# Two layer norms and four small jobs move from VectorE to ScalarE, and decayed reads stay in PSUM, in a gated delta-rule attention kernel with a mixture-of-experts layer

## The chip, the cores and the metric

One core of a Trainium2 chip (trn2) runs one program. The metric is the device time of that program in microseconds (us). The engines are TensorE (PE; PEld is its weight load), VectorE (DVE), ScalarE (ACT), GpSimd (POOL) and SyncE (SP, the DMA queue). Each runs its own instruction stream in order and meets the others only at semaphores.

## The reference

One transformer layer over 4096 tokens of width 256, in fp32. First comes a linear attention with 8 heads and 8 modes per head, then a top-2 mixture of 8 experts.

```python
h = layernorm(x) * (1 + ca) + sa
q, k, v = h @ Wq, h @ Wk, h @ Wv                   # 8 heads of 64
beta, tg = sigmoid(h @ Wbeta), sigmoid(h @ Wtg)    # per head and mode
rho = exp(-softplus(log_decay)); g = log(clip(tg * rho, 1e-6))
# q, k rotated by pos * exp(omega_log_scale) * inv_freq, unit length
for t in range(T):                                 # per head and mode
    S = S * exp(g[t])
    dv = (v[t] - k[t] @ S) * beta[t]
    S = S + outer(k[t], dv)
    y[t] = q[t] @ S
o = einsum(y, softmax(mode_logits)) * sigmoid(h @ Wg)
x = x + ga * (o @ Wo)
h2 = layernorm(x) * (1 + cb) + sb
x = x + gb * moe(h2)                               # top 2 of 8, capacity 1024
```

## The kernel before

The attention runs over 32 tiles of 128 tokens. A tile is done in two halves (`hh` = 0 and 1), each with 8 of the 16 "quads" of head and mode. Half `u = 2n + hh` works on two things at once. It builds its own chunk systems: angles, rotated keys and queries, decays, Gram matrices, and a triangular inverse for 4 chunks of 32 tokens. And it runs the recurrence of the half before it, `v = u - 1`, chunk by chunk. `memories(step, c)` in VectorE's `half` marks the recurrence steps; c is the chunk.

One chunk of the recurrence is a chain over engines. PE reads the memories (`memory_read`, L572) into `bank_mem[g]`, g = 0 and 1. VectorE scales that read by the decay (L1263) and subtracts it from the values (L1266): `right_sides`. PE multiplies by the inverse (L589) and adds the reads of the outputs (L595): `corrections`. VectorE scales by `dec_end` (L1273), PE forms the update (L608), POOL fades the state (L1561) and VectorE adds (L1282).

The work of the half itself is placed between those steps by hand. What the change touches sits here:

- `beta_decays` (L1199) first copies the last decay of each chunk into `dec_end` (L1201), then makes `bd` (L1205), just ahead of the fourth `right_sides`.
- At the end of a half VectorE runs `solve` (L1234): a transpose (L1236), 31 elimination steps j of two instructions each (L1245, L1247), a transpose into `tt` (L1250). `meanwhile` puts small jobs between the steps.
- In an hh = 1 half `tile_norm(n + 1)` (L1096) comes before `solve`: ScalarE's square root (L788), reciprocal (L1098), normalised rows `xn` (L1099). PE's `tile_front` turns `xn`, ScalarE makes `hT` (L753, L755) and the sigmoid `sg` (L759), and inside the same `solve` VectorE runs `clip_decays` at j = 8 (L1104 copies the betas, L1105 clips), `sum_decays` at j = 16 (the scan L1110, the spread over modes L1111) and `weigh_decays` at j = 24 (L1116).
- In an hh = 0 half `residual(n - 1)` (L1291 to L1295) and `second_norm(n - 1)` (L1297: square root L870 on ScalarE, L1299, `xn2` L1301) come before `solve`. PE's `route` (L633, L638) turns `xn2`, ScalarE makes `h2T` (L896), PE makes the router's logits, and VectorE takes them at j = 12 of that `solve` (`take_logits`, L1306).
- ScalarE's `roots` (L793) takes the squared lengths that PE sums in `sum_squares` (L490) from POOL's `squares` (L1552): a logarithm (L798) and an exponential (L799). POOL starts that work after `pw_raw`, which VectorE raises after the residual: L1586, two products and a sum (L1523, L1526), then `squares`.

ScalarE loads a function table (ACT_TABLE_LOAD) where two functions of different tables follow each other. After the tile loop come the routing of all tokens and the experts' matmuls, which the change does not touch.

Of the kernel before, what the change touches and what calls it, by code (L numbers as in the profile page):

```python
# [17 lines left out]
ALU = mybir.AluOpType  # L18
# [3 lines left out]
P = 128  # L22
# [101 lines left out]
def build(nc, x_in, Wq, Wk, Wv, Wbeta, Wtg, mode_logits, log_decay, omega_log, Wg, Wo,  # L124
# [12 lines left out]
    with outer, ctx:  # L137
        names = {}

        def sem(name):  # L140
# [8 lines left out]
            "vector": dict.fromkeys(["xn_ready", "xn2_ready", "dve_bank_free0", "dve_bank_free1", "state_ready0", "state_ready1",  # L149
# [4 lines left out]
            "scalar": dict.fromkeys(["act_bank_free0", "act_bank_free1", "hid_ready0", "hid_ready1",  # L154
# [151 lines left out]
        V_STEPS = (95, 190)  # L306
# [122 lines left out]
        def _(pe):  # L429
# [226 lines left out]
            def half(n, hh, first=False, last=False):  # L656
# [71 lines left out]
        def _(act):  # L728
# [19 lines left out]
            def tile_front(n):  # L748
# [10 lines left out]
                take(lambda b: act.activation(sg[:], b[:, 0:P], ACT.Sigmoid))  # L759
# [24 lines left out]
            def front(n, hh):  # L784

                if hh == 0:
                    act.wait_ge(sem("var_ready"), n + 1)
                    act.activation(stat[:, 8:9], stat[:, 7:8], ACT.Sqrt, bias=eps_ln[:]).then_inc(sem("std_ready"), 1)  # L788
                    tile_front(n)
# [3 lines left out]
            def roots(n, hh):  # L793
# [4 lines left out]
                take(lambda b: act.activation(rn[:].rearrange("p h t -> p (h t)"), b[:, :], ACT.Ln, bias=eps_l2[:]))  # L798
# [26 lines left out]
            def half(n, hh, first=False, last=False):  # L825
# [26 lines left out]
                act.activation(gc_end[:, hh], gc_end[:, hh], ACT.Exp).then_inc(sem("gc_end_ready"), 1)  # L852
                act.activation(eg_col[:, hh], col[:, :, 0, hh * HQ:hh * HQ + HQ], ACT.Exp).then_inc(sem("eg_col_ready"), 1)
# [14 lines left out]
                if hh == 0 and not first:  # L868
                    act.wait_ge(sem("var2_ready"), n)
                    act.activation(stat2[:, 8:9], stat2[:, 7:8], ACT.Sqrt, bias=eps_ln[:]).then_inc(sem("std2_ready"), 1)  # L870
# [10 lines left out]
                if not last:  # L881
                    front(*after(n, hh))
                if hh == 0 and not first:
                    route(n - 1)
                if not last:
                    roots(*after(n, hh))
# [17 lines left out]
            front(0, 0)  # L904
# [14 lines left out]
            act.wait_ge(sem("var2_ready"), NT)  # L919
            act.activation(stat2[:, 8:9], stat2[:, 7:8], ACT.Sqrt, bias=eps_ln[:]).then_inc(sem("std2_ready"), 1)  # L920
# [5 lines left out]
        def _(dve):  # L926
# [169 lines left out]
            def tile_norm(n):  # L1096
                dve.wait_ge(sem("std_ready"), n + 1)
                ln(dve.reciprocal(stat[:, 9:10], stat[:, 8:9]))  # L1098
                vec(dve.tensor_scalar(xn[:], xt[:], stat[:, 6:7], stat[:, 9:10], ALU.subtract, ALU.mult), "xn_ready", n + 1)  # L1099

            def clip_decays(n):
                dve.wait_ge(sem("sg_ready"), n + 1)
                dve.wait_ge(sem("rho_ready"), 1)
                ln(dve.tensor_copy(gb[64:128, :], sg[64:128, :]))  # L1104
                vec(dve.tensor_scalar(sg[0:64, :], sg[0:64, :], rho[0:64], 1e-6, ALU.mult, ALU.max), "tg_clipped", n + 1)  # L1105

            def sum_decays(n):
# [3 lines left out]
                vec(dve.tensor_tensor(xg[:], gb[:].rearrange("p (c j) -> p c j", c=NC).unsqueeze(2).broadcast_to([P, NC, 4, C]),  # L1111
                                      of_mode.unsqueeze(1).unsqueeze(3).broadcast_to([P, NC, 4, C]), ALU.mult), "spread_ready", n + 1)

            def weigh_decays(n):
                dve.wait_ge(sem("eg_raw"), n + 1)
                vec(dve.tensor_scalar(ew[0:64, :], ew[0:64, :], w_col[0:64], None, ALU.mult), "eg_ready", n + 1)  # L1116


# [80 lines left out]
            def beta_decays(u, hh):  # L1199
                dve.wait_ge(sem("dec_ready"), u + 1)  # L1200
                ln(dve.tensor_copy(dec_end[:, hh], dec[:, :, :, C - 1]))  # L1201
# [50 lines left out]
            def right_sides(v, hh, c):  # L1252
# [6 lines left out]
                for g in range(2):  # L1259
# [36 lines left out]

            def second_norm(t):  # L1297
                dve.wait_ge(sem("std2_ready"), t + 1)
                ln(dve.reciprocal(stat2[:, 9:10], stat2[:, 8:9]))  # L1299
                dve.wait_ge(sem("rows_sent"), since("rows_sent", t))  # L1300
                vec(dve.tensor_scalar(xn2[:], xr[:], stat2[:, 6:7], stat2[:, 9:10], ALU.subtract, ALU.mult), "xn2_ready", t + 1)  # L1301
# [72 lines left out]
            def half(n, hh, first=False, last=False):  # L1374
# [62 lines left out]
            tile_norm(0)  # L1437
            clip_decays(0)
            sum_decays(0)
            weigh_decays(0)  # L1440
# [403 lines left out]
```

## Time and profile before

| | us |
|---|---|
| time, 3 runs | 7270.02, 7274.76, 7275.66; median 7274.76 |
| profiled execution: its time | 7273.93 |
| its span | 7272.2 |
| busy PE, PEld | 4621.0 (64%), 3991.4 (55%) |
| busy DVE | 5425.6 (75%) |
| busy ACT | 3286.5 (45%) |
| busy POOL | 2786.6 (38%) |
| mean granted TensorE clock | 0.793 |

Busy times count what an engine executed, not its waits. "Granted clock" is the share of TensorE's full clock that the chip gave it. A timeline row has the start, the duration, engine, line, operation, output<-inputs with their shape, and in brackets the idle time before it with what ended that idle time. A group row has the count, the busy sum, the mean ns of one, and the idle time before them. Times inside the rows are microseconds from the span's start.

### The profile page before, as it was taken

To read this page: it belongs to the slowest core of one execution; us is meant where nothing else is said; L and a number is where in the kernel's file an instruction comes from. 1 tells how busy PE (TensorE), PEld (TensorE's weight loads), DVE (VectorE), ACT (ScalarE), POOL (GpSimd) and SP (SyncE) were. 2 spreads that over 40 slices of the span, in tenths; PEclk is the share of its full clock that TensorE was granted. 3 is DMA by queue.
4 is the path that set the end of the run, shared out by engine and by line. 5 is a ranking of instruction groups with operands and counts; after the bars stand their busy time and mean duration, and the time that the engine had idled before them with its cause. 6 is when DMAs were issued, how large, how long until landed. Compare 5 with 4: busy or idle time off the path is not lost. (4 is left out here: it accounts for less than half of the span.)

```text
span 7272.2 us, 195759 instructions
## 1 busy us (share of the span) xinstructions
PE 4621.0 (64%) x78513; PEld 3991.4 (55%) x78513; DVE 5425.6 (75%) x10088; ACT 3286.5 (45%) x5497; POOL 2786.6 (38%) x1789
## 2 busy tenths in 40 slices
PE   1666666666666666666666666666666666664994
PEld 1555555556555555555655555655565555563662
DVE  4888888888888888888888888888888888883003
ACT  1445454445444455444544445454454444541220
POOL 3444343344433434434434344343443434433003
PEclk6778877778777787777877778778787777886997
DMA  2000000000000000000000000000000000002223
GB/s 85 2 5 5 5 5 5 5 5 5 2 5 5 5 5 5 5 5 5 5 2 5 5 5 5 5 5 5 5 5 2 5 5 5 5 25 93 69 69 101
DMA packets 77478, 109.70 MB, mean 15 GB/s; under 512 B 20576, under 2 KB 66208, under 8 KB 75424
## 3 DMA queue, kind: packets, MB, share of 16 engines
q1 hardware_dynamic: 67616, 71.42, 3.1%
q0 software_dynamic: 8960, 25.39, 1.2%
q8 instruction: 672, 11.01, 0.6%
q14 instruction: 230, 1.88, 0.1%
HBM read 57.89 MB, written 38.89 MB: 13 GB/s over the span
## 5 line engine op out<-in xcount | busy, mean ns | idle before, releaser
L1561 POOL TENSOR_TENSOR state<-state,gc_end 128x512 f32<-128x512 f32 x512 | 594.7, 1173 | 1647.8 <-PE bank L595 1607.4
L589 PE MATMUL bank<-rhs,te 128*64 128x64 f32 x8192 | 432.2, 262 | 1054.3 <-DVE rhs L1266 725.5
L589 PEld LDWEIGHTS bank<-rhs,te 128*64 128x64 f32 x8192 | 360.4, 170 | 1141.1 <-DVE rhs L1266 1092.4
L572 PEld LDWEIGHTS bank<-state,ke 128*64 128x64 f32 x16384 | 610.5, 159 | 385.9 <-issue 194.6
L572 PE MATMUL bank<-state,ke 128*64 128x64 f32 x16384 | 649.7, 247 | 265.1 <-DVE outT L1284 171.7
L608 PE MATMUL last_two<-dvs,kte 128*64 128x64 f32 x16384 | 699.7, 250 | 179.3 <-DVE dvs L1273 179.3
L766 ACT ACTIVATE te<-tt 32x256 f32<-32x256 f32 x1024 | 421.9, 412 | 815.6 <-DVE tt L1250 805.1
L608 PEld LDWEIGHTS last_two<-dvs,kte 128*64 128x64 f32 x16384 | 637.7, 163 | 195.5 <-DVE dvs L1273 186.4
L1247 DVE TENSOR_TENSOR last_two<-last_two,prod 128x31 f32<-128x31 f32 (+15 forms) x1984 | 692.8, 349 | 68.1
L808 ACT ACTIVATE ke<-kq 32x512 f32<-32x512 f32 x1024 | 642.8, 628 | 198.6 <-DVE kq L1197 184.9
L1245 DVE TENSOR_TENSOR prod<-bd,last_two 128x31 f32<-128x31 f32 (+15 forms) x1984 | 670.6, 338 | 69.9
L533 PE MATMUL bank<-kq,ke 128*64 128x64 f32 x16384 | 615.7, 245 | 123.3 <-DVE pw L1232 112.0
L533 PEld LDWEIGHTS bank<-kq,ke 128*64 128x64 f32 x16384 | 594.5, 160 | 131.5 <-DVE pw L1232 77.2
L773 ACT ACTIVATE kte<-kt 32x512 f32<-32x512 f32 x1024 | 641.4, 626 | 15.8 <-PE last_two L608 1.9
L1586 POOL TENSOR_TENSOR pw<-pw,w_quad 128x1024 f32<-128x1024 f32 x64 | 122.4, 1913 | 1122.2 <-DVEq L1422 1122.2
L781 ACT ACTIVATE dv<-bank 128x256 f32<-128x256 f32 x512 | 188.5, 380 | 747.7 <-DVE dvs L1273 738.2
L508 PE MATMUL bank<-row_group,select 128*128 128x128 f32 x3072 | 431.2, 296 | 32.9 <-DVE col L1160 27.7
L1282 DVE TENSOR_TENSOR state<-last_two,state 128x512 f32<-128x512 f32 x512 | 354.0, 691 | 127.2 <-POOL state L1561 89.3
L508 PEld LDWEIGHTS bank<-row_group,select 128*128 128x128 f32 x3072 | 389.7, 203 | 52.4 <-DVE col L1160 28.0
L1756 DVE TENSOR_TENSOR yrow<-last_two,b_row 128x256 f32<-128x256 f32 x64 | 27.2, 425 | 508.5 <-PE last_two L1710 508.5
L595 PE MATMUL bank<-qg,state 128*64 128x32 f32 x8192 | 401.2, 249 | 0.0
L1574 POOL TENSOR_TENSOR tmp<-raw,cos_t 128x1024 f32<-128x1024 f32 x64 | 151.7, 2370 | 590.8 <-ACTq L849 590.8
(254 smaller groups left out, 10392.7 us busy)
## 6 DMA issues: line engine op xcount, KB each, us to landing
w_sb<-in_L_ffn_W_dram SPq DMA_DIRECT2D x16, 1024.0 KB, 9.4
expert_rows<-ke SPq DMA_DIRECT2D x1, 8192.0 KB, 21.9
xrows<-expert_rows SPq DMA_DIRECT2D x16, 512.0 KB, 8.4
expert_outputs<-yrow POOLq DMA_DIRECT2D x16, 512.0 KB, 3.4
xt<-_attn_hidden_states_dram SPq DMA_DIRECT2D x32, 128.0 KB, 2.1
xr<-_attn_hidden_states_dram SPq DMA_DIRECT2D x32, 128.0 KB, 2.1
x_after_attention<-xr SPq DMA_DIRECT2D x32, 128.0 KB, 1.7
xo<-x_after_attention SPq DMA_DIRECT2D x32, 128.0 KB, 3.6
```

What stands on the lines that cost most here:

```text
L508: mm = pe.matmul(b[:, ql * P:ql * P + P], select[:, b4 * 4 + ql, :], row_group[:, group, :], start=True, stop=True)
L533: mm = pe.matmul(b[s, q * 2 * C:(q + 1) * 2 * C], ke[:, c, r, q, s], kq[:, r, q, :, c * C:c * C + C], start=(r == 0), stop=(r == 1))
L572: mm = pe.matmul(bank_mem[g][s, q % 4 * DK:q % 4 * DK + DK], ke[:, c, r, q, s], state[:, hh * HQ + q, r, :], start=(r == 0), stop=(r == 1))
L589: pe.matmul(bank_mem[g][s, q % 4 * DK:q % 4 * DK + DK], te[:, q, s], rhs[:, q, :], start=True, stop=True)
L595: mm = pe.matmul(out_bank(g, side), state[:, hh * HQ + q, r, :], qg[:, r, q, c * C:c * C + C], start=(j == 0 and r == 0), stop=False)
L608: mm = pe.matmul(bank_upd[g][s, (q % 4) * P + r * DK:(q % 4) * P + r * DK + DK], kte[:, r, q, s], dvs[:, q, :], start=True, stop=True)
L766: ins = act.activation(te[s, :, 32 * m:32 * m + 32], tt[s, c, :, :], ACT.Copy)
L773: ins = act.activation(kte[s, :, :, 32 * m:32 * m + 32].rearrange("p r q f -> p (r q) f"), kt[s, :, :, c * C:c * C + C].rearrange("p r q f ...
L808: ins = act.activation(ke[s, c, :, :, 32 * m:32 * m + 32].rearrange("p r q j -> p (r q) j"), kq[s, :, :, 0, c * C:c * C + C].rearrange("p ...
L1245: ln(dve.tensor_tensor(pr, a_prob[:, j + 1:C, j:j + 1].broadcast_to([P, rows, cols]), t_prob[:, j:j + 1, 0:cols].broadcast_to([P, rows, co ...
L1247: ln(dve.tensor_tensor(below, below, pr, ALU.subtract))
L1561: pool.tensor_tensor(sv, sv, gc_end[:, vh, 4 * g:4 * g + 4, c].unsqueeze(2).broadcast_to([P, 4, 2 * DK]), ALU.mult).then_inc(sem(f"state_f ...
```

## The change

- `tile_norm` and `second_norm` run on ScalarE: ln(var + eps), the negated mean, exp of -0.5 times the logarithm, their product, and one Identity activation with scale and bias. VectorE keeps the statistics.
- `tile_norm(n + 1)` stands on ScalarE behind `clear_inverse`, ahead of the copies of the values. `second_norm(n - 1)` stands inside `roots`: its logarithm ahead of the logarithm of the lengths, the rest behind that.
- Since `route` needs `xn2`, it moves behind `roots` on ScalarE and behind `sum_squares` on PE. `take_logits` stays at j = 12 on VectorE.
- The sigmoid is split by partitions: decays' half to `sg`, betas' half straight to `gb`.
- ScalarE spreads the decays (four copies with a scale) and multiplies by the mode weights, behind its exponential of the summed decays.
- ScalarE copies `dec_end` behind its exponential of the decays.
- `right_sides` writes the scaled read back into `bank_mem[g]` and subtracts from there.

```diff
@@ PE and ScalarE, end of a half
-                if hh == 0 and not first:
-                    route(n - 1)
-                if not last:
-                    sum_squares(u + 1)
+                if not last:
+                    sum_squares(u + 1)
+                if hh == 0 and not first:
+                    route(n - 1)
...
+            def tile_norm(n):
+                act.wait_ge(sem("var_ready"), n + 1)
+                act.activation(stat[:, 8:9], stat[:, 7:8], ACT.Ln, bias=eps_ln[:])
+                act.activation(stat[:, 10:11], stat[:, 6:7], ACT.Copy, scale=-1.0).then_inc(sem("std_ready"), 1)
+                act.wait_ge(sem("std_ready"), 3 * n + 1)
+                act.activation(stat[:, 9:10], stat[:, 8:9], ACT.Exp, scale=-0.5).then_inc(sem("std_ready"), 1)
+                act.wait_ge(sem("std_ready"), 3 * n + 2)
+                act.activation(stat[:, 11:12], stat[:, 10:11], ACT.Copy, scale=stat[:, 9:10]).then_inc(sem("std_ready"), 1)
+                act.wait_ge(sem("std_ready"), 3 * n + 3)
+                act.activation(xn[:], xt[:], ACT.Identity, scale=stat[:, 9:10], bias=stat[:, 11:12]).then_inc(sem("xn_ready"), 1)
+            def second_norm(t, root=None):
+                act.wait_ge(sem("var2_ready"), t + 1)
+                act.activation(stat2[:, 8:9], stat2[:, 7:8], ACT.Ln, bias=eps_ln[:])
+                act.activation(stat2[:, 10:11], stat2[:, 6:7], ACT.Copy, scale=-1.0).then_inc(sem("std2_ready"), 1)
+                if root:
+                    root()
...
+                act.wait_ge(sem("rows_sent"), since("rows_sent", t))
+                act.activation(xn2[:], xr[:], ACT.Identity, scale=stat2[:, 9:10], bias=stat2[:, 11:12]).then_inc(sem("xn2_ready"), 1)
...
-                take(lambda b: act.activation(sg[:], b[:, 0:P], ACT.Sigmoid))
+                act.activation(sg[0:64, :], bank_act[turns.bank()][0:64, 0:P], ACT.Sigmoid)
+                take(lambda b: act.activation(gb[64:128, :], b[64:128, 0:P], ACT.Sigmoid))
...
                     act.wait_ge(sem("g_summed"), n + 1)
                     act.activation(ew[0:64, :], gb[0:64, :], ACT.Exp).then_inc(sem("eg_raw"), 1)
+                    for m in range(4):
+                        ins = act.activation(xg[:, :, m, :], gb[:].rearrange("p (c j) -> p c j", c=NC), ACT.Copy, scale=of_mode[:, m:m + 1])
+                    ins.then_inc(sem("spread_ready"), 1)
+                    act.wait_ge(sem("eg_raw"), n + 1)
+                    act.activation(ew[0:64, :], ew[0:64, :], ACT.Copy, scale=w_col[0:64]).then_inc(sem("eg_ready"), 1)
...
+                act.wait_ge(sem("dec_ready"), u + 1)
+                act.activation(dec_end[:, hh], dec[:, :, :, C - 1], ACT.Copy)
...
-                ln(dve.tensor_tensor(rhs[:, of], ksv, eg_col[:, hh, c, of].unsqueeze(2).broadcast_to([P, 4, DK]), ALU.mult))
+                ln(dve.tensor_tensor(ksv, ksv, eg_col[:, hh, c, of].unsqueeze(2).broadcast_to([P, 4, DK]), ALU.mult))
...
-                    vec(dve.tensor_tensor(r4, vv, r4, ALU.subtract), f"rhs_ready{g}", vc + 1)
+                    vec(dve.tensor_tensor(r4, vv, ksv.rearrange("p (h g) v -> p h g v", g=2), ALU.subtract), f"rhs_ready{g}", vc + 1)
...
-                if hh == 0 and not first:
-                    second_norm(n - 1)
-                if hh == 1 and not last:
-                    tile_norm(n2)
                 meanwhile = {}
                 if hh == 1 and not last:
-                    meanwhile.update({8: [lambda: clip_decays(n2)], 16: [lambda: sum_decays(n2)], 24: [lambda: weigh_decays(n2)]})
+                    meanwhile.update({8: [lambda: clip_decays(n2)], 16: [lambda: sum_decays(n2)]})
                 if hh == 0 and not first:
                     meanwhile[12] = [lambda: take_logits(n - 1)]
```

ScalarE's stream at the end of the loop's hh = 0 half, before: the take of `unit`, the two `h2T` of `route`, then the logarithm and exponential of `rn`.

```order
L790 ACTIVATE unit<-bank 128x512 [waits act_bank_full]
L745 REGISTER_ALU
L743 REGISTER_ALU [waits act_bank_free0]
L896 ACTIVATE h2T<-bank,mod_col 128x128 [waits act_bank_full]
L743 REGISTER_ALU [waits act_bank_free1]
L896 ACTIVATE h2T<-bank,mod_col 128x128 [waits act_bank_full]
L745 REGISTER_ALU
L743 REGISTER_ALU [waits act_bank_free0]
L798 ACT_TABLE_LOAD
L798 ACTIVATE rn<-bank,eps_l 128x512 [waits act_bank_full]
L799 ACT_TABLE_LOAD
L799 ACTIVATE rn<-rn 128x512 [waits act_bank_free1]
```

And with the change (`stat` is `stat2` and `xn` is `xn2` here; L763 to L773 are `second_norm`, L828 the logarithm and L833 the exponential of `rn`, L936 is `h2T`):

```order
L763 ACT_TABLE_LOAD [waits act_bank_free0]
L763 ACTIVATE stat<-stat,eps_ln 128x1 [waits var2_ready]
L764 ACTIVATE stat<-stat 128x1
L743 REGISTER_ALU
L828 ACTIVATE rn<-bank,eps_l 128x512 [waits act_bank_full]
L767 ISA [waits act_bank_free1]
L768 ACT_TABLE_LOAD
L768 ACTIVATE stat<-stat 128x1 [waits std2_ready]
L769 REGISTER_ALU
L770 ACTIVATE stat<-stat 128x1 [waits std2_ready]
L771 REGISTER_ALU
L773 ACTIVATE xn<-xr,stat 128x256 [waits rows_sent,std2_ready]
```

The activation that makes `xn2` now stands behind the logarithm of `rn`, and `h2T` behind both.

PE's stream at the same place, before:

```order
L555 MATMUL bank<-hT,wg_sb 128x128 x8
L452 REGISTER_ALU
L482 MATMUL bank<-hT,wqk_sb 128x128 x8
L633 MATMUL bank<-cmat,xn 128x128
L452 REGISTER_ALU
L633 MATMUL bank<-cmat,xn 128x128
L638 MATMUL bank<-wr_sb,h2T 128x8 x2
L490 MATMUL bank<-rhs,cmat 128x512
```

And with the change:

```order
L555 MATMUL bank<-hT,wg_sb 128x128 x8
L452 REGISTER_ALU
L482 MATMUL bank<-hT,wqk_sb 128x128 x8
L490 MATMUL bank<-rhs,cmat 128x512
L452 REGISTER_ALU
L633 MATMUL bank<-cmat,xn 128x128 x2
L638 MATMUL bank<-wr_sb,h2T 128x8 x2
```

The turning of `xn2` (L633) and the logits (L638) now stand behind `sum_squares` (L490).

## Rows read from the trace of the kernel before

**Rows 1.** The engines' busy time in three stretches: the tile loop, and two short ones.

```profile
core 0: us, PE busy (x) PEld busy (x) DVE busy (x) ACT busy (x) POOL busy (x), PEclk, DMA share, GB/s
100.00:6900.00 6800.00, 4351.37 (x77549) 3811.73 (x77550) 5303.26 (x9805) 3217.43 (x5396) 2697.61 (x1687) 0.79 0.03 10
3190.50:3195.50 5.00, 2.51 (x78) 2.40 (x79) 4.38 (x8) 4.88 (x9) 4.84 (x3) 1.00 0.01 3
3199.30:3203.00 3.70, 3.70 (x69) 3.58 (x67) 1.73 (x3) 2.20 (x5) 1.05 (x1) 0.50 0.02 4
```

**Rows 2.** A VectorE line that runs once a tile: durations, first and last start.

```profile
L1094 DVE TENSOR_SCALAR pos<-pos x3: 226/226/228, 2906.8 to 3309.5; 128x128 f32<-128x128 f32 x3
```

**Rows 3.** VectorE's groups by line and shape.

```profile
L1201 DVE COPY dec_end<-dec 128x32 f32<-128x32 f32 x64 | 66.9, 1045 | 9.6 <-DVE outT L1284 9.4
...
L1105 DVE TENSOR_SCALAR sg<-sg,rho 64x128 f32<-64x128 f32 x32 | 29.5, 921 | 1.1
...
L1247 DVE TENSOR_TENSOR last_two<-last_two,prod 128x256 f32<-128x256 f32 x64 | 27.6, 432 | 2.2
...
L1111 DVE TENSOR_TENSOR xg<-gb,cmat 128x512 f32<-128x512 f32 x32 | 22.1, 691 | 1.1
...
L1116 DVE TENSOR_SCALAR ew<-ew,w_col 64x128 f32<-64x128 f32 x32 | 8.9, 278 | 3.5 <-ACT ew L802 2.4
```

**Rows 4.** Line L1266 alone: duration in ns (min/median/max).

```profile
L1266 DVE TENSOR_TENSOR rhs<-v_sb,rhs x512: 424/425/2009, 230.8 to 6606.7; 128x256 f32<-128x256 f32 x171
```

**Rows 5.** Timeline, all engines, fourth chunk of a half (start us, us, what).

```profile
3194.84 2.41 POOL L1581 TENSOR_TENSOR kq<-tmp 128x1024 f32<-128x1024 f32 x1
...
3195.53 2.00 DVE L1266 TENSOR_TENSOR rhs<-v_sb,rhs 128x256 f32<-128x256 f32 x1
...
3199.31 3.66 PE L533 MATMUL bank<-kq,ke 128*64 128x64 f32 x64
...
3203.02 0.42 DVE L1231 TENSOR_TENSOR cos_t<-bank,bd 128x256 f32<-128x256 f32 x1 [1.92 <-PE bank L533]
```

**Rows 6.** Timeline, all engines, end of an hh = 1 half.

```profile
3115.16 0.42 DVE L1232 TENSOR_TENSOR pw<-bank,dec 128x256 f32<-128x256 f32 x1
...
3117.41 0.60 ACT L874 ACTIVATE v_sb<-bank 128x512 f32<-128x512 f32 x1 [1.13 <-PE bank L544]
...
3121.87 1.96 DVE L1236 STREAM_TRANSPOSE bd<-cos_t 128x1024 f32<-128x1024 f32 x1
...
3126.38 0.28 ACT L759 ACTIVATE sg<-bank 128x128 f32<-128x128 f32 x1
...
3129.58 0.94 DVE L1105 TENSOR_SCALAR sg<-sg,rho 64x128 f32<-64x128 f32 x1
```

**Rows 7.** Timeline, all engines, end of an hh = 0 half.

```profile
3017.40 0.18 DVE L1295 BATCH_NORM_AGGREGATE stat<-stat 128x2 f32<-128x6 f32 x1 [0.15 <-DVE stat L1293]
...
3019.81 2.01 DVE L1236 STREAM_TRANSPOSE bd<-cos_t 128x1024 f32<-128x1024 f32 x1
...
3026.09 1.04 POOL L1552 TENSOR_TENSOR rhs<-unit 128x512 f32<-128x512 f32 x1
...
3027.18 2.07 PE L490 MATMUL bank<-rhs,cmat 128*128 128x512 f32 x2 [1.49 <-POOL rhs L1552]
...
3029.30 0.69 ACT L798 ACTIVATE rn<-bank,eps_l 128x512 f32<-128x512 f32 x1 [2.87 <-PE bank L490]
...
3030.00 1.28 ACT L799 ACT_TABLE_LOAD   x1
...
3030.91 0.17 DVE L1306 TENSOR_TENSOR lg<-bank,br_row 128x8 f32 x1
...
3031.30 0.63 ACT L799 ACTIVATE rn<-rn 128x512 f32<-128x512 f32 x1
```

**Rows 8.** ScalarE's groups by line and shape.

```profile
L753 ACT ACTIVATE hT<-bank,mod_col 128x128 f32<-128x128 f32 x64 | 29.3, 457 | 90.4 <-PE bank L467 84.5 <-ACT hT L755 5.8
...
L870 ACT ACTIVATE stat<-stat,eps_ln 128x1 f32<-128x1 f32 x31 | 9.1, 294 | 234.8 <-DVE stat L1295 234.8
```

**Rows 9.** Timeline, the last tile's logits (idle before: from `xn2` on).

```profile
6624.51 0.17 DVE L1306 TENSOR_TENSOR lg<-bank,br_row 128x8 f32<-128x8 f32 x1 [2.60 <-PE bank L638]
```

More of the change, by code:

```diff
@@ L305, in build @@
         DVE_TURNS = (13, 26)
-        V_STEPS = (95, 190)
+        V_STEPS = (92, 185)
         G_STEPS = (29, 26)
@@ L746, in take, with tile_front @@
                 turns.next()
-            def tile_front(n):
+            def tile_norm(n):
[14 more added lines that the diff above has]
+                    root()
+                act.wait_ge(sem("std2_ready"), 3 * t + 1)
+                act.activation(stat2[:, 9:10], stat2[:, 8:9], ACT.Exp, scale=-0.5).then_inc(sem("std2_ready"), 1)
+                act.wait_ge(sem("std2_ready"), 3 * t + 2)
+                act.activation(stat2[:, 11:12], stat2[:, 10:11], ACT.Copy, scale=stat2[:, 9:10]).then_inc(sem("std2_ready"), 1)
+                act.wait_ge(sem("std2_ready"), 3 * t + 3)
+                act.wait_ge(sem("rows_sent"), since("rows_sent", t))
+                act.activation(xn2[:], xr[:], ACT.Identity, scale=stat2[:, 9:10], bias=stat2[:, 11:12]).then_inc(sem("xn2_ready"), 1)
+            def tile_front(n, first):
                 for k in range(KC):
@@ L758, in tile_front @@
                     act.sem_inc(sem("hT4_ready"), 1)
-                take(lambda b: act.activation(sg[:], b[:, 0:P], ACT.Sigmoid))
+                if not first:
+                    act.wait_ge(sem("groups_ready"), n)
+                act.wait_ge(sem("act_bank_full"), turns.uses() + 1)
+                act.activation(sg[0:64, :], bank_act[turns.bank()][0:64, 0:P], ACT.Sigmoid)
+                take(lambda b: act.activation(gb[64:128, :], b[64:128, 0:P], ACT.Sigmoid))
                 act.sem_inc(sem("sg_ready"), 1)
@@ L782, in take_dv, with front, roots @@
                                    ).then_inc(sem(f"dv_ready{g}"), 1)
-            def front(n, hh):
+            def front(n, hh, first=False):
                 if hh == 0:
-                    act.wait_ge(sem("var_ready"), n + 1)
-                    act.activation(stat[:, 8:9], stat[:, 7:8], ACT.Sqrt, bias=eps_ln[:]).then_inc(sem("std_ready"), 1)
-                    tile_front(n)
+                    tile_front(n, first)
                 take(lambda b: act.activation(unit[:].rearrange("p h t -> p (h t)"), b[:, :], ACT.Copy))
                 act.sem_inc(sem("raw_ready"), 1)
-            def roots(n, hh):
+            def roots(n, hh, t=None):
                 if hh == 0:
@@ L797, in roots, with logarithm @@
                     act.activation(gb[0:64, :], sg[0:64, :], ACT.Ln).then_inc(sem("g_ready"), 1)
-                take(lambda b: act.activation(rn[:].rearrange("p h t -> p (h t)"), b[:, :], ACT.Ln, bias=eps_l2[:]))
+                def logarithm():
+                    take(lambda b: act.activation(rn[:].rearrange("p h t -> p (h t)"), b[:, :], ACT.Ln, bias=eps_l2[:]))
+                if t is None:
+                    logarithm()
+                else:
+                    second_norm(t, logarithm)
                 act.activation(rn[:], rn[:], ACT.Exp, scale=-0.5).then_inc(sem("rn_root"), 1)
@@ L867, in half @@
                 clear_inverse(v, first)
-                if hh == 0 and not first:
-                    act.wait_ge(sem("var2_ready"), n)
-                    act.activation(stat2[:, 8:9], stat2[:, 7:8], ACT.Sqrt, bias=eps_ln[:]).then_inc(sem("std2_ready"), 1)
+                if hh == 1 and not last:
+                    tile_norm(n + 1)
                 if not first:
@@ L882, in half @@
                     front(*after(n, hh))
+                if not last:
+                    roots(*after(n, hh), t=n - 1 if hh == 0 and not first else None)
                 if hh == 0 and not first:
                     route(n - 1)
-                if not last:
-                    roots(*after(n, hh))
                 if not first:
@@ L902, in gaps @@
                 act.activation(per_tile[:, 5, t0:t1], per_tile[:, 4, t0:t1], ACT.Exp).then_inc(sem("gap_exp"), 1)
-            front(0, 0)
+            tile_norm(0)
+            front(0, 0, first=True)
             roots(0, 0)
@@ L918, in _ @@
                     next_expansions(v, c + 1)
-            act.wait_ge(sem("var2_ready"), NT)
-            act.activation(stat2[:, 8:9], stat2[:, 7:8], ACT.Sqrt, bias=eps_ln[:]).then_inc(sem("std2_ready"), 1)
+            second_norm(NT - 1)
             route(NT - 1)
@@ L1094, in tile_stats @@
                 ln(dve.tensor_scalar(pos[:], pos[:], float(P), None, ALU.add))
[L1096 to L1099, printed above, removed]
             def clip_decays(n):
@@ L1295, in residual @@
                 vec(dve.bn_aggr(stat2[:, 6:8], stat2[:, 0:6]), "var2_ready", t + 1)
[L1297 to L1301, printed above, removed]
             def take_logits(t):
```

14 lines of the change are left out of this document (2 added, 12 removed).

## The prediction

> **What bounds the kernel now.** I read the engines' busy times in stretches first. In the tile loop (100 to 6900 us) VectorE is busy 5303 of 6800 us, PE 4351, ScalarE 3217, POOL 2698 [rows 1]. One line that runs once a tile starts three times in 402.7 us, so a tile takes 201.35 us [rows 2], and 31 such tiles (each an hh = 1 half and the hh = 0 half of the next tile) make 6242 us of the span. Next I read the timeline of two halves, all engines together. VectorE has next to no gap there. Where it stands still, it is for a named partner: the Gram matrix of PE in the fourth chunk, 1.92 us [rows 5], and the square root ahead of the solve. So VectorE's own stream, with those waits, sets the time, and what leaves that stream counts in full until a partner becomes late. Each part is priced by asking who is late next.
>
> **First norm, end of the hh = 1 half.** Today L1232 ends at 3115.16 + 0.42 = 3115.58 and the transpose L1236 starts at 3121.87 [rows 6]. In the 6.29 us between lie a wait for ScalarE, a reciprocal and L1099. Afterwards nothing stands between the two but the usual 0.04: **6.25 us less**. Who could be late next is `clip_decays` at j = 8, which needs the sigmoid. Its turn comes at about 3123.1 (7.5 us into the solve, as today). On ScalarE the norm now stands ahead of the copies of the values, so `xn` is ready before PE asks for it; PE's turning, `hT` and the sigmoid follow the values directly. Today the sigmoid ends at 3126.66 [rows 6], some 4.8 us behind `xn`, which ends as L1236 starts; counted from the end of the last copy of the values (L874, 3118.01 [rows 6]) it ends near 3122.8. That just fits, and a miss costs tenths.
>
> **Small jobs in that solve.** L1111 (0.69 us) and L1116 (0.28) leave VectorE [rows 3]; the copy L1104 of the same 64x128 shape as L1116 leaves too and is taken at the same 0.28. With the gaps that is **1.3 us less**. L1105 stays. On ScalarE the spread is four copies of 128x128 with a scale, each at most the 0.46 of L753 [rows 8], so under 2 us. PE needs it for `columns`, but the scan that starts it comes 7 us sooner than today, so PE gets it sooner too. This costs nothing; were the cover gone, it would cost those 2 us a tile.
>
> **Fourth chunk, both halves.** The copy L1201 leaves VectorE: 1.05 us on average for 32 elements [rows 3]. It starts while POOL works and ends with POOL's instruction. The subtraction L1266 takes 0.42 us in the median and 2.01 at most [rows 4]; the long one is in the fourth chunk, starts at 3195.53 and ends at 3197.53, and POOL's L1581 ends at 3194.84 + 2.41 = 3197.25 [rows 5]. It reads two tensors from SBUF; afterwards it reads one from PSUM, like L1247, whose mean of 0.43 [rows 3] leaves no room for such waits. So VectorE gets 1.05 + 1.58 = 2.6 us. The partner behind is PE: its Gram matrix L533 starts at 3199.31 [rows 5], and it needs the rotated queries that L1581 makes. It can't start before 3197.3, so the path gets **2.0 us less in a half, 4.0 in a tile**. The bounds are 0 (another partner late) and 2.6 in a half; the row of POOL's end decides for 2.0. ScalarE's copy of `dec_end`, 32 elements, lies behind its exponentials, and its reader is a half away: nothing.
>
> **Writing the scaled read into its bank.** The same shape written to PSUM takes 0.432 us (L1247 [rows 3]) against 0.424 [rows 4]: 16 instructions a tile, **0.1 us more**.
>
> **Second norm, end of the hh = 0 half.** The statistics end at 3017.58; L1236 starts at 3019.81 [rows 7], and would start at 3017.61: 2.2 us less. But `take_logits` is still at j = 12 of this solve. Its turn was 3030.91 [rows 7] and would be 3028.7. The logits need `xn2`, and `xn2` now stands on ScalarE behind the logarithm of the lengths. That one waits for PE's sum (3027.18 to 3029.25), which waits for POOL's squares, which end at 3027.13 [rows 7] and hang on `pw_raw`; nothing in the change moves them. So: table load for the exponential from 3030.00, 1.28 us [rows 7]; two activations on one column at 0.29 each (L870 [rows 8], its like); one of 128x256, between 0.46 (128x128, L753 [rows 8]) and 0.69 (128x512, L798 [rows 7]), taken at 0.57; two waits of ScalarE for itself, an estimate of 0.17 each from VectorE's 0.15 ahead of L1295 [rows 7]. That makes `xn2` ready at 3032.8. From `xn2` to the logits the last tile shows 2.60 us [rows 9], so 3035.4. The solve stands still for 6.7 us at j = 12, and everything behind is 3035.4 - 3030.9 = **4.5 us later** than today instead of 2.2 sooner (bounds 3.9 and 5.3, by the ends of the terms). Behind this wait on VectorE is the rest of the elimination; nobody else gets late. SP's later store of `xn2` and load of `xr` have most of a tile to spare.
>
> The load L799 takes 1.28 us and a second one (L798's) stands just before it in the same tile. The Trainium skill, page "ScalarE: Activation LUTs", section "Table sets: the hidden batching unit", says that one set holds both exp and ln, so ln then exp would need a single load. By it the exponential's load would be missing and the time 31 x 1.28 = 40 us lower. The built stream has that load, and the trace disagrees with the rule. The same page, "What ACT_TABLE_LOAD costs", adds about 1.38 us of drain to the 1.28; by it the time would be 43 us higher. No such 1.38 us shows: L799's activation starts at 3031.30, 0.02 us behind the load [rows 7].
>
> **Sum.** Per tile -6.25 - 1.3 - 4.0 + 0.1 + 4.5 = -6.95 us; times 31 it is -215 us. The last hh = 1 half gives 2.0 more; the first and the last norm have nothing beside them and cost some 2.3 us each on ScalarE (a load more and two columns). Together -213. Against the profiled execution's 7273.93 us that is 7061, and against the median, 0.8 us above it, **7062 us**.
>
> **The rivals.**
> 1. *PE keeps its clock in the fourth chunk.* In 3190.5 to 3195.5 the granted clock is 1.00, and in 3199.3 to 3203.0 it is 0.50, where the Gram matrix takes 3.66 us; in between PE stood idle for want of L1266 [rows 1, 5]. If PE comes to it with shorter gaps and the clock stays up, L533 takes about half, and VectorE, which waits for it, gets up to 1.8 us more in each of 63 halves: 113 us, to 6950. Against it: PE still waits for POOL's queries, over a microsecond. 0.24.
> 2. *The fourth chunk gives nothing*, because another partner (`ke` on ScalarE, the update) takes the place: 63 x 2.0 = 126 us back, 7188. 0.10.
> 3. *The logits don't hold the solve*: 31 x 6.7 = 208 us less, 6854. This needs the squares to come 7 us sooner; their queue on POOL is unchanged. 0.05.
> 4. *One load for ln and exp*: 7022, by the row's 1.28 us for a load that falls away. Two loads show in the trace. 0.02.
> 5. *Slower: the logits' wait eats everything.* Place: L1306 at j = 12. Each microsecond that the logits come later than 3035.4 costs 31 us, so it decides from 3042.3 on, 6.9 us later than worked out; at 3044 the time is 7329. For it speaks that the chain from the sum of squares to the logits crosses between PE, ScalarE and VectorE six times and waits for itself on ScalarE, and each of these steps was taken from another place. Against it, no row shows such a step at over a microsecond beyond its work. The Trainium skill's same page, "Rules for kernel authors", wants multiply and add on VectorE, not on ScalarE, which speaks against the whole change. Here ScalarE is busy 47% of the loop and gets about 6 us of 201 more. 0.05.
> 6. *Nothing that can be measured* (gains and wait cancel): the wait would be 13.6 instead of 6.7 us. 0.02.
>
> **How the numbers follow.** The forecast has the remaining 0.52; its own range, from the bounds of the logits' term (3.9 to 5.3 us) and of the chunk's (1 to 2.6 us in a half), is 7005 to 7150. For 8 in 10 the range takes in rival 1 and its spread below and half of rival 2 above: 6930 to 7170. What a measurement of this kernel can tell from no change is about 0.2%, 15 us. Faster by more: 0.52 + 0.24 + 0.10 + 0.05 + 0.02 = 0.93; within: 0.02; slower: 0.05.
>
> **What would show it.** In the profile after, VectorE goes from its last `pw` to the transpose without a gap in hh = 1 halves; the logits' line waits some 6.5 us for PE in each of 31 tiles, near 200 us in all; the line after L1266 has a maximum near its median; the Gram matrix starts right behind POOL's last rotated sum; the line that runs once a tile comes every 194.4 us. I am wrong if the logits' wait is missing or over 10 us, or if the Gram matrix's wait grows by what the subtraction gave.

## The result and the profile after

| | before | after |
|---|---|---|
| time, median of 4 runs each | 7273.83 us | 7002.59 us (6999.14 to 7012.93) |
| ratio, 95% interval | | 0.963 (0.9616 to 0.9645) |
| span of the profiled execution | 7272.2 | 6997.4 |
| busy VectorE | 5425.6 | 5135.8 |
| busy ScalarE | 3286.5 | 3430.8 |
| busy PE | 4621.0 | 4452.0 |

The kernel is 271 us faster; 213 were forecast. Between the two profiled executions it is 274.8 us, and nearly all of that lies in the tile loop: from the first start of the transpose ahead of the solve to its last (64 starts, L1236 before, L1261 after) pass 6330.5 us before and 6059.7 after, 270.8 less. I call this the loop's time below. I compare by it where 10 us matter, since the experts' stage behind the loop, which no run touches, waits 504 to 509 us on one line in six of the profiled executions and 472 to 476 in the other eight (VectorE for PE's last products). The ratios below leave out two slow executions, one of `e6_before_bank_only` at 14515 us and one of `e9_sbuf_pe_kept_busy` at 7372.

VectorE's waits after (line waited for: us in all, times, longest):

```profile
DVE lg L1325 <- PE bank L638: 208.2, 32, 7.0
...
DVE cos_t L1256 <- PE bank L533: 85.3, 69, 6.9
...
DVE sg L1139 <- ACTq L791: 26.1, 16, 9.2
```

The first is the forecast one, 6.7 us in each of 31 tiles; 202.5 us of it stand in those tiles, 6.5 in each, and the rest in the last tile's row behind the loop. The second was 126.4 us before. The third is new: 9.2 us of it are one wait at the start of the kernel, the other 16.9 are 15 waits of at most 1.2 us.

Single lines after, the subtraction (answering to [rows 4]) and the scan of the decays (durations min/median/max in ns):

```profile
L1291 DVE TENSOR_TENSOR rhs<-v_sb,bank x512: 420/420/423, 228.7 to 6334.1; 128x256 f32<-128x256 f32 x171
L1144 DVE TENSOR_TENSOR_SCAN gb<-cmat,gb x32: 416/1552/2311, 124.8 to 6090.0; 64x128 f32<-64x128 f32 x32
```

The line that runs once a tile starts 32 times between 111.0 and 6066.8 us, so a tile takes 192.1 us on average; the forecast had 194.4. No subtraction reaches 2 us any more. But the scan, which the change does not touch, went from a mean of 416 ns to 1652.

The fourth chunk after, beside [rows 5]:

```profile
3060.52 2.37 POOL L1592 TENSOR_TENSOR tmp<-raw,sin_t 128x1024 f32<-128x1024 f32 x1
...
3062.41 0.42 DVE L1291 TENSOR_TENSOR rhs<-v_sb,bank 128x256 f32<-128x256 f32 x1
...
3062.96 2.37 POOL L1593 TENSOR_TENSOR kq<-tmp 128x1024 f32<-128x1024 f32 x1
...
3065.56 2.08 PE L533 MATMUL bank<-kq,ke 128*64 128x64 f32 x64 [1.53 <-POOL kq L1593]
```

The subtraction takes 0.42 us beside POOL's L1592 and is over before L1593 starts. The Gram matrix starts 0.23 us behind L1593 and takes 2.08 us instead of 3.66. Busy times and granted clock in that stretch (columns as in [rows 1]):

```profile
3065.60:3067.60 2.00, 2.00 (x65) 1.93 (x65) 1.09 (x3) 1.17 (x3) 2.00 (x2) 1.00 0.04 8
```

The clock is 1.00 (2.4 GHz) where [rows 1] has 0.50 (1.2 GHz). Over the 63 halves that run a recurrence, the first Gram matrix lasts 3.58 us on average before (all over 3 us) and 2.16 after (1 over 3 us), and it starts 2.06 us behind POOL's end before and 0.24 after.

The second norm and the logits after, beside [rows 7]:

```profile
3092.07 1.04 POOL L1564 TENSOR_TENSOR rhs<-unit 128x512 f32<-128x512 f32 x1
3093.17 2.07 PE L490 MATMUL bank<-rhs,cmat 128*128 128x512 f32 x2 [4.04 <-POOL rhs L1564]
...
3095.28 0.69 ACT L828 ACTIVATE rn<-bank,eps_l 128x512 f32<-128x512 f32 x1 [3.74 <-PE bank L490]
3096.07 1.28 ACT L768 ACT_TABLE_LOAD   x1
...
3097.36 0.20 ACT L768 ACTIVATE stat<-stat 128x1 f32<-128x1 f32 x1
...
3097.93 0.60 ACT L773 ACTIVATE xn<-xr,stat 128x256 f32<-128x256 f32 x1
...
3101.54 0.17 DVE L1325 TENSOR_TENSOR lg<-bank,br_row 128x8 f32 x1 [6.95 <-PE bank L638]
```

From the end of POOL's squares (3093.11) to the logits pass 8.43 us; the forecast had 3035.4 - 3027.13 = 8.27.

Where the time went, as means over the 31 tiles, from the starts of VectorE's lines in the timeline:

| stretch, us per tile | before | after | difference | forecast |
|---|---|---|---|---|
| hh = 1: last `pw` to transpose (first norm) | 6.71 | 0.58 | -6.13 | -6.25 |
| hh = 1: the solve | 28.51 | 28.74 | +0.23 | -1.3 |
| both: rotation to first Gram's use (fourth chunk) | 51.09 | 44.51 | -6.58 | -4.0 |
| hh = 0: last `pw` to transpose (second norm) | 5.17 | 3.09 | -2.08 | -2.2 |
| hh = 0: transpose to logits | 11.10 | 17.41 | +6.31 | +6.7 |
| the rest | | | -0.4 | +0.1 |

They sum to -8.65 us, by 31 -268. The difference of the chunk's stretch is 3.3 us in a half.

### The profile page after: what moved, and what is told of

It reads as the page before. It is cut to its first block and busy times, and to the rows that moved or that the text cites. A ratio compares the mean times of both kernels' runs of the same rounds, so it can differ in the third digit from the quotient of the medians.

```text
span 6997.4 us, 195918 instructions
## 1 busy us (share of the span) xinstructions
PE 4452.0 (64%) x78513; PEld 3830.1 (55%) x78513; DVE 5135.8 (73%) x9800; ACT 3430.8 (49%) x6010; POOL 2767.8 (40%) x1789
## 5 line engine op out<-in xcount | busy, mean ns | idle before, releaser
L589 PE MATMUL bank<-rhs,te 128*64 128x64 f32 x8192 | 412.6, 254 | 765.9 <-DVE rhs L1291 490.0
L572 PE MATMUL bank<-state,ke 128*64 128x64 f32 x16384 | 656.1, 248 | 341.0 <-DVE outT L1309 221.4
L572 PEld LDWEIGHTS bank<-state,ke 128*64 128x64 f32 x16384 | 616.8, 160 | 415.8 <-DVE state L1307 237.1
L589 PEld LDWEIGHTS bank<-rhs,te 128*64 128x64 f32 x8192 | 345.0, 163 | 844.4 <-DVE rhs L1291 795.8
L608 PE MATMUL last_two<-dvs,kte 128*64 128x64 f32 x16384 | 658.9, 241 | 180.1 <-DVE dvs L1298 180.1
L608 PEld LDWEIGHTS last_two<-dvs,kte 128*64 128x64 f32 x16384 | 597.2, 154 | 196.5 <-DVE dvs L1298 187.3
L533 PE MATMUL bank<-kq,ke 128*64 128x64 f32 x16384 | 536.2, 227 | 199.8 <-DVE pw L1257 111.2
L533 PEld LDWEIGHTS bank<-kq,ke 128*64 128x64 f32 x16384 | 512.6, 142 | 214.0 <-issue 125.8
L508 PEld LDWEIGHTS bank<-row_group,select 128*128 128x128 f32 x3072 | 375.7, 198 | 47.7 <-DVE col L1186 24.2
L595 PE MATMUL bank<-qg,state 128*64 128x32 f32 x8192 | 374.4, 240 | 0.0
```

The costliest lines, as they stand in the source:

```text
L508: mm = pe.matmul(b[:, ql * P:ql * P + P], select[:, b4 * 4 + ql, :], row_group[:, group, :], start=True, stop=True)
L533: mm = pe.matmul(b[s, q * 2 * C:(q + 1) * 2 * C], ke[:, c, r, q, s], kq[:, r, q, :, c * C:c * C + C], start=(r == 0), stop=(r == 1))
L572: mm = pe.matmul(bank_mem[g][s, q % 4 * DK:q % 4 * DK + DK], ke[:, c, r, q, s], state[:, hh * HQ + q, r, :], start=(r == 0), stop=(r == 1))
L589: pe.matmul(bank_mem[g][s, q % 4 * DK:q % 4 * DK + DK], te[:, q, s], rhs[:, q, :], start=True, stop=True)
L595: mm = pe.matmul(out_bank(g, side), state[:, hh * HQ + q, r, :], qg[:, r, q, c * C:c * C + C], start=(j == 0 and r == 0), stop=False)
L608: mm = pe.matmul(bank_upd[g][s, (q % 4) * P + r * DK:(q % 4) * P + r * DK + DK], kte[:, r, q, s], dvs[:, q, :], start=True, stop=True)
```

## The experiments

Each ratio is against executions of the kernel before that were measured together with the run; the kernel after is at 0.963. "Loop" is the loop's time against that of the kernel named.

**Is the logits' wait worth 6.5 us a tile?** `e1_logits_j20` takes them eight steps later:

```diff
-                    meanwhile[12] = [lambda: take_logits(n - 1)]
+                    meanwhile[20] = [lambda: take_logits(n - 1)]
```

> The changed kernel with the logits taken at j = 20 instead of j = 12. If the wait at j = 12 (208 us in all) holds VectorE up and nothing hides behind it, the logits' line waits for nothing and the time falls by about 31 x 6.3 = 195 us, to 6808. If VectorE's wait only covers another one (the rest of the half waits for PE or ScalarE anyway), less than 50 us comes back and a new wait shows at the start of the next half.

Measured: 0.9364 (0.9349 to 0.938), loop 187.6 us less than after. The waits list has no row of the logits for PE left. The wait was on the path with 188 of its 202 us. Of the rest, 11 us lie in the other halves' solve, 0.37 us longer in each of 31 (29.11 us against 28.74).

**Does the second norm's move pay?** `e2_norm2_back` gives it back to VectorE, with `Sqrt` and the old order on PE and ScalarE:

```diff
@@ VectorE
+                if hh == 0 and not first:
+                    second_norm(n - 1)
                 meanwhile = {}
...
```

> The changed kernel with the second norm, and the order of the router behind it, as before: square root on ScalarE, reciprocal and normalised rows on VectorE, the rest changed. If this part of the change is a loss by its order (it gave 2.1 us and costs 6.3 a tile), the time falls by 31 x 4.2 = 130 us, to 6872. If moving work off VectorE pays here too, it rises by up to 31 x 2.1 = 65 us, to 7068.

Measured: 0.9469 (0.9453 to 0.9485), loop 114.1 us less than after. So this part alone costs 3.7 us a tile; the table's +6.31 - 2.08 says 4.2.

**What are the fourth chunk's 3.3 us a half made of?** `e3_reads_in_sbuf` writes the decayed reads to SBUF again:

```diff
-                    ln(dve.tensor_tensor(ksv, ksv, eg_col[:, hh, c, of].unsqueeze(2).broadcast_to([P, 4, DK]), ALU.mult))
+                    ln(dve.tensor_tensor(rhs[:, of], ksv, eg_col[:, hh, c, of].unsqueeze(2).broadcast_to([P, 4, DK]), ALU.mult))
...
-                    vec(dve.tensor_tensor(r4, vv, ksv.rearrange("p (h g) v -> p h g v", g=2), ALU.subtract), f"rhs_ready{g}", vc + 1)
+                    vec(dve.tensor_tensor(r4, vv, r4, ALU.subtract), f"rhs_ready{g}", vc + 1)
```

> The changed kernel with the scaled read written to SBUF again, so that the subtraction reads two tensors there. Both theories expect the last subtraction of the fourth chunk to end with POOL's rotated sum again, at 2.0 us, and the Gram matrix to start 2 us later: 63 x 2.0 = 126 us, 7129. Clock theory (the chunk gave 3.3 us in a half instead of 2.0 because PE now comes to the Gram matrix at full clock): PE's clock is at 0.5 there again, its 64 matmuls take 3.6 us instead of 2.1, and the loss is 63 x 3.3 = 205 us, 7208. Rival (the surplus comes from VectorE's own stream): 7129, the Gram matrix still at 2.1 us.

Measured: 0.9853 (0.9837 to 0.987), loop 165.4 us more than after, 2.6 in a half. The subtraction is back at 2 us, and so is the slow Gram matrix:

```profile
3139.78 2.00 DVE L1291 TENSOR_TENSOR rhs<-v_sb,rhs 128x256 f32<-128x256 f32 x1
...
3143.56 3.27 PE L533 MATMUL bank<-kq,ke 128*64 128x64 f32 x64
```

On average it lasts 3.27 us (55 of 63 over 3 us) and starts 2.06 us behind POOL's end again. The chunk's stretch is 3.0 us longer in a half; the two solves are 0.7 us a tile shorter in exchange. The other direction is `e6_before_bank_only`, the kernel before with the same two lines of the change and nothing else.

> The kernel before with nothing but the decayed reads kept in their bank. Theory A (the fourth chunk's gain comes from the lock with GpSimd going and TensorE keeping its clock for the Gram, and needs no other part of the change): the 512 instructions of the subtraction fall to 420 ns, the first Gram to about 2.1 us, each half loses 2.0 to 3.3 us: 126 to 210 us less than the kernel before, ratio 0.971 to 0.983. Rival B (the clock is kept only since ScalarE and VectorE reach this place in another rhythm with the other parts): the Gram stays at 3.1 to 3.7 us and the gain at 100 to 130 us, ratio 0.982 to 0.986.

Measured: 0.9739 (0.9721 to 0.9756), loop 202.7 us less than before; the Gram matrix at 2.16 us. The chunk's stretch is 3.0 us shorter in a half, 185 us in all. The other 17 lie in the hh = 1 solve (27.97 us against 28.51), where the clip L1105 falls from a mean of 921 ns to 356. Theory A near its upper end: two lines hold three quarters of what the whole change brought.

`e4_dec_end_back` leaves the bank part and gives only the copy of `dec_end` back to VectorE:

```diff
-                act.wait_ge(sem("dec_ready"), u + 1)
-                act.activation(dec_end[:, hh], dec[:, :, :, C - 1], ACT.Copy)
...
                 dve.wait_ge(sem("dec_ready"), u + 1)
+                ln(dve.tensor_copy(dec_end[:, hh], dec[:, :, :, C - 1]))
```

> The changed kernel with the copy of dec_end on VectorE again, ahead of the fourth chunk's right sides. PE's corrections come 1.2 us later, but its Gram matrix waits for POOL's rotated queries anyhow. If the idle time before the corrections decides the clock (2.7 us in one piece instead of 1.5), the Gram matrix takes 3.6 us again: 63 x 1.5 = 95 us, 7098. If not, it takes 2.1 us and the time rises by under 15 us, 7003 to 7018. Rival (VectorE's own stream decides, not PE): all of the 1.2 us counts, 63 x 1.2 = 75 us, with the Gram matrix at 2.1 us.

Measured: 0.9702 (0.9685 to 0.9718), loop 57.7 us more than after: 0.9 in a half of the 1.19 that the copy lasts there. No theory holds as it was put. The Gram matrix starts 0.84 us behind POOL's end instead of 0.24, so PE now comes later than POOL, and it lasts 2.51 us on average instead of 2.16 (10 of 63 over 3 us).

**Is it TensorE's clock?** `e9_sbuf_pe_kept_busy` is e3 with matmuls of constants where TensorE waits for the right side. They compute nothing that is used:

```diff
+                if c == 3:
+                    for k in range(24):
+                        pe.matmul(bank_upd[0][:, 0:64], same_norm, cmat[:, 0:64], start=True, stop=True)
```

> The kernel with the decayed reads in SBUF again (the run with ratio 0.985), and 24 matmuls more on TensorE in every half, of constants into a bank that the next update overwrites, put where TensorE waits 2.7 us for the fourth chunk's first right side. By the projection's rows they last some 1.7 us, so they fit into that wait and compute nothing that is used. Theory A (the Gram's 3.1 us are TensorE at 1.2 GHz, since it stood idle before it, and not the reads' place): the first Gram falls to 2.1 to 2.4 us, the halves lose 0.7 to 1.1 us each: 45 to 75 us less than without them, ratio 0.975 to 0.979. Rival B (the Gram is slow since its operands lie in a memory that VectorE and GpSimd use at the same time): the Gram stays at 3.1 us, and the time is the same or longer, ratio 0.984 to 0.990.

Measured: 1.0029 (1.0003 to 1.0056), slower than e3; its executions spread from 7260 to 7332 us. The filling does not last 1.7 us but 5.57 in 45 halves and 10.50 in 19, 7.0 on average (the expectation of the next run has 5.76, which is wrong), and it holds the corrections up. Yet the Gram matrix falls from 3.27 to 2.30 us, none of 63 over 3. The time tells nothing here, the duration does. `e12_sbuf_pe_short_fill` has the right size:

```diff
+                    for k in range(10):
+                        for s in SIDES:
+                            pe.matmul(bank_upd[0][s, 0:64], same_norm[:, s], cmat[:, 0:64], start=True, stop=True)
```

> The same question as in the run before with the 24 matmuls of constants, which lasted 5.76 us a half on average and not 1.7, so that they held the corrections up. Now 20 matmuls of half the width (64 columns of the weights), which by the reads' rows (32 such matmuls in 2.1 us) last 1.3 us at the full clock and 2.6 at half of it, inside the wait of 2.75 us. Theory A (the Gram's 3.1 us are TensorE's lower clock, given by its idleness before): the first Gram lasts 2.1 to 2.4 us again, now with nothing held up, and 40 to 75 us go against the kernel with the decayed reads in SBUF: ratio 0.975 to 0.980. Rival B (the longer work before the Gram, and not a clock, made it fast there): the Gram goes back to 2.9 to 3.3 us and the ratio stays at 0.983 to 0.988. Rival C (the clock comes back, but what follows the Gram waits for GpSimd or VectorE, so nothing is won): the Gram at 2.1 to 2.4 us and a ratio of 0.981 to 0.987.

Measured: 0.9816 (0.98 to 0.9832), loop 30.8 us less than e3. The filling and the Gram matrix in one half (the trace has two rows for each fp32 matmul, so 20 show as 40 and the Gram matrix's 32 as 64):

```profile
3119.27 1.37 PE L587 MATMUL last_two<-cmat 128*64 128x64 f32 x40
...
3125.67 2.06 PE L533 MATMUL bank<-kq,ke 128*64 128x64 f32 x64
```

and the granted clock over that Gram matrix, then over the one of e3 above:

```profile
3125.90:3128.00 2.10, 2.10 (x67) 2.03 (x63) 2.03 (x3) 0.00 (x0) 1.05 (x1) 1.00 0.00 0
```

```profile
3143.60:3146.70 3.10, 3.10 (x68) 3.10 (x66) 2.04 (x3) 1.32 (x3) 1.05 (x1) 0.57 0.03 5
```

More work ahead of it makes the Gram matrix shorter, 2.43 us on average (8 of 63 over 3), so what TensorE does before it sets its clock: theory A for the mechanism. The ratio is rival C's: the Gram matrix ends 1.33 us earlier, but VectorE uses it only 0.88 us earlier in a half (55 us), since in 39 of the 63 it is by then still busy with its own work. And the stretch from the transpose to the logits is 0.56 us longer in each of 31 tiles (17 us): the logits' releaser did not move along, and VectorE waits longer for it.

**Why does the solve not gain its 1.3 us?** `e5_scan_j20`:

```diff
-                    meanwhile.update({8: [lambda: clip_decays(n2)], 16: [lambda: sum_decays(n2)]})
+                    meanwhile.update({8: [lambda: clip_decays(n2)], 20: [lambda: sum_decays(n2)]})
```

> The changed kernel with one edit: the running sum of the decays (L1144) is worked four steps later in the solve, at step 20 instead of 16. Theory A (the scan's 1652 ns instead of 416 is the port it shares with GpSimd, which at step 16 works on the high turns, and not a slower instruction): at step 20 GpSimd's high turns are over or between two instructions in many tiles, the mean of L1144 falls towards 416 ns, and 1.2 us a tile go: 20 to 40 us less than the changed kernel, ratio to the kernel before 0.958 to 0.960. Rival B (the scan is slower since its input comes from another engine's write, or it waits for the clipped decays): its mean stays at 1.6 us and the time within 10 us of the changed kernel, ratio 0.962 to 0.964.

Measured: 0.9582 (0.9569 to 0.9595), loop 32.2 us less than after, and

```profile
L1144 DVE TENSOR_TENSOR_SCAN gb<-cmat,gb x32: 416/416/417, 124.8 to 6062.8; 64x128 f32<-64x128 f32 x32
```

Theory A: the same instruction takes 416 ns four steps later. In the kernel after it stands beside POOL and ends 0.29 us behind POOL's instruction, though it would take only 0.42 by itself. I call such a wait the lock:

```profile
3004.58 2.34 POOL L1538 TENSOR_TENSOR tmp<-tmp,kq 128x1024 f32<-128x1024 f32 x1
...
3005.28 1.93 DVE L1144 TENSOR_TENSOR_SCAN gb<-cmat,gb 64x128 f32<-64x128 f32 x1
```

The Trainium skill, "SBUF — State Buffer", section "SBUF: two separate sides", says that VectorE with two SBUF inputs and GpSimd exclude each other for a whole instruction. These rows agree for the scan, and e3 with after for the subtraction.

`e10_norm1_back` gives the first norm back to VectorE, with its `Sqrt`:

```diff
+                if hh == 1 and not last:
+                    tile_norm(n2)
                 meanwhile = {}
```

> The changed kernel with the first norm on VectorE and its root as Sqrt again, all else changed. Theory A (the first norm's move is a gain of its own, as its stretch shows: 6.7 to 0.6 us from the last product to the solve): each odd half is 6.1 us longer, 31 times, 175 to 205 us more than the changed kernel; ratio 0.987 to 0.991. Rival B (ScalarE's own work for the norm delays something there, so part of it comes back): 120 to 170 us more, ratio 0.979 to 0.986.

Measured: 0.984 (0.9825 to 0.9856), loop 159.8 us more than after: rival B's size, but VectorE gives the part back. The stretch ahead of the solve is 6.13 us longer, and the solve 1.78 shorter (26.96 us against 28.74, and 28.51 before), which makes 135 us; the rest lies in the other solve and in the fourth chunk, some 0.4 us a tile each. The scan is at a mean of 468 ns.

With the norm in front, the solve is 28.51 - 26.96 = 1.55 us shorter than before. The removed instructions are 1.3 of it (L1104 0.22, L1111 0.69, L1116 0.28 us and three gaps of 0.04); the clip's mean fell from 921 to 622 ns besides. Without the norm in front the solve starts 6.1 us earlier against POOL and ScalarE, the scan falls beside POOL, and the clip waits for the sigmoid.

**Which order is best?** `e7_norm2_first` puts `second_norm` and `route` ahead of the lengths' sum and logarithm on ScalarE and PE:

```diff
@@ PE
+                if hh == 0 and not first:
+                    route(n - 1)
                 if not last:
                     sum_squares(u + 1)
-                if hh == 0 and not first:
-                    route(n - 1)
@@ ScalarE
+                if hh == 0 and not first:
+                    second_norm(n - 1)
+                    route(n - 1)
                 if not last:
-                    roots(*after(n, hh), t=n - 1 if hh == 0 and not first else None)
-                if hh == 0 and not first:
-                    route(n - 1)
+                    roots(*after(n, hh))
```

> The changed kernel with the second norm and the logits' transposes and products put ahead of the sums of the keys' squares and their logarithm on ScalarE and TensorE, the logits still taken at step 12. Theory A (the 6.5 us of the logits' wait are the work on the keys' lengths that stands between the norm's logarithm and its end): the logits come some 5 us earlier, VectorE waits 1 to 2 us for them, and 120 to 170 us go against the changed kernel; ratio 0.940 to 0.947. The keys' lengths come later in exchange and need a third table load in the half; if GpSimd's or VectorE's first step after the solve waits for them (rival B), the stretch from the last step of the solve to the next chunk is longer by 1 to 3 us in these halves and only 30 to 110 us go; ratio 0.948 to 0.959.

Measured: 0.9461 (0.9447 to 0.9476), loop 123.3 us less than after; the logits' wait falls from 202 to 73 us (2.4 each). That is as good as taking the second norm back, and less than moving the logits. `e8_later_small_jobs` moves all three jobs (logits 12 to 20, clip 8 to 12, scan 16 to 20).

> The changed kernel with all three small jobs of VectorE in the solve put later: the logits at step 20 instead of 12, the clipping of the decays at 12 instead of 8, their sum at 20 instead of 16. If the three delays add (theory A): the logits give about 190 us as they did alone, the sum up to 38, the clipping's waits and its lock up to 40: 200 to 260 us less than the changed kernel, ratio 0.927 to 0.936. If the delays are not independent (rival B: what waits there has its releaser moved along, or GpSimd's work lies under the new places too), the time is that of the logits alone, within 10 us of 190 less, ratio 0.935 to 0.938.

Measured: **0.929 (0.9277 to 0.9302)**, median 6779.34 against 7294.16 us, loop 238.9 us less than after. Theory A: logits alone 187.6, scan alone 32.2, which leaves 19 for the clip. That is a remainder, since no run moves the clip alone: its wait for the sigmoid went from 26.1 to 9.2 us, but its own mean from 632 to 964 ns. The best version of all. `e11_later_norm2_back` is the same with the second norm on VectorE.

> The version with the three small jobs put later (ratio 0.929), with the second norm on VectorE again. Theory A (once the logits are taken late enough, moving the second norm is the gain of 2.1 us a tile that its removed instructions are): 55 to 75 us more than that version, ratio 0.936 to 0.940. Rival B (the norm costs ScalarE as much as it saves VectorE, so with the logits late both are alike): within 15 us, ratio 0.927 to 0.931.

Measured: 0.939 (0.9377 to 0.9403), loop 69.3 us more than e8, 2.2 a tile. Theory A: the second norm's move is a gain of its 2.1 us once the logits are taken late, and a loss of 3.7 at step 12.

## Why the prediction was right, and where it was off

**What bounds the kernel**: right. The table's stretches of VectorE would sum to the loop's time whatever bounds it; what shows it are e1, e2 and e10, where 188 of 202 us of a wait, 114 of 130 and 160 of some 190 in VectorE's stream came through.

**First norm, -6.25**: -6.13 measured. That a late sigmoid "costs tenths" was right in size (16.9 us in the loop, 0.55 a tile), but it was not the only cost of starting the solve earlier.

**Small jobs, -1.3**: mis-sized, +0.23 measured. The removed instructions do bring their 1.3 (e10). I moved the scan 6 us against POOL's sum L1538 and left its 416 ns as they were, though the subtraction in [rows 4, 5] shows what POOL does to an instruction with two SBUF inputs. It measured +1.24 for the scan; e5 shows the cause. The waits for the sigmoid add 0.55, and the clip's shorter mean (921 to 632 ns) takes 0.3 off.

**Fourth chunk, -2.0 a half**: mis-sized, -3.3 measured. The lock's part stands: the subtraction is 1.58 shorter, the copy 1.05, and PE's Gram matrix starts 1.8 us sooner against POOL's end. What I left to rival 1, with a chance of 0.24, happened: the clock stayed up, 62 of 63 first Gram matrices took under 3 us, and one is 1.42 us shorter on average. 1.8 + 1.4 is 3.2. My argument against it, that PE would still wait over a microsecond for POOL, was a true reading (1.53 us) and no reason: what changed is the work before that wait. PE's corrections in the half of [rows 5], and the first of them after:

```profile
3195.09 0.69 PE L589 MATMUL bank<-rhs,te 128*64 128x64 f32 x16 [2.44 <-DVE rhs L1266]
...
3197.58 1.12 PE L589 MATMUL bank<-rhs,te 128*64 128x64 f32 x16 [1.36 <-DVE rhs L1266]
```

```profile
3061.96 0.69 PE L589 MATMUL bank<-rhs,te 128*64 128x64 f32 x16 [1.51 <-DVE rhs L1291]
```

After, PE does not wait ahead of the second correction, which takes 0.67 us, not 1.12. So the clock was down by the second correction before (0.50 from 3197.6 to 3198.6 us), and between the reads of the memories (L572) and the Gram matrix TensorE stood idle for 3.80 us there against 3.04 after (1.51 and 1.53). How much idleness, and where it must lie, costs the clock stays open.

**Bank write, +0.1**: 432 ns as taken.

**Second norm and logits, +4.5**: +4.2 measured; wait 6.7 us forecast and 6.5 measured (202.5 us in 31 tiles). In the tile shown, `xn2` is ready 5.41 us behind POOL's squares where 5.64 were worked out, and from there to the logits pass 3.02 us instead of 2.60. Rivals 3 and 5 are out.

**Rival 4**, one load for logarithm and exponential: out. L768's load of 1.28 us stands right behind L828's logarithm, and its activation 0.01 us behind the load, so neither claim of the Trainium skill, "ScalarE: Activation LUTs", holds here: not the single load (section "Table sets: the hidden batching unit"), nor the drain (section "What ACT_TABLE_LOAD costs").

**The sum**: the two mis-sized terms are -1.3 x 63 = -82 and +1.5 x 31 = +47 us; the other terms together make the remaining -24, of which the table's rest is -16, and the forecast of 7062 becomes 7003. That is 2 us below the plain forecast's own range of 7005 to 7150 and inside the wide one. Part of this closeness is luck: the two errors have opposite signs, and without the solve's the time would be near 6956, where rival 1 had 6950.

## What to carry to other kernels

When a job leaves the engine that bounds, the jobs behind it move in time against the other engines: check what each of them will then stand beside (a lock) and whether what it takes will be ready (a releaser that does not move). Moving where a result is taken costs one number; three such moves were worth almost as much as the whole change (239 against 271 us), and the logits' alone 188. A stall ahead of matmuls is paid twice when TensorE comes out of it at half its clock.

## What the runs showed of the hardware

- The Gram matrix's matmuls behind a stalled stretch ran at a granted clock of 0.50 and 0.57 in the two rows shown instead of 1.00: their 64 rows took 3.66 and 3.27 us instead of 2.08. 20 matmuls of constants in the gap, 1.37 us, brought the mean from 3.27 to 2.43 us.
- A 64x128 scan, 416 ns by itself, took up to 2311 ns beside POOL, and ended 0.29 us behind POOL's instruction in the row shown. The 128x256 subtraction took 2.0 us with both inputs in SBUF and at most 423 ns with one in PSUM.
- The mean granted clock was 0.793 before, 0.817 after and 0.829 in e8, but it doesn't rank the kernels: e12 has 0.824 at 7134 us.
